# Re-ordering an edge layer's pipeline beside a dense product: two parts a step instead of three, the sum of messages last, and two masks weighted one tile ahead

## The chip, the cores and the metric

The kernel runs on one core of one Trainium2 chip. The metric is the device time of one execution in microseconds (us), taken as the median of the runs shown. TensorE (PE in the rows) does the matrix products and the transposes, VectorE (DVE) and ScalarE (ACT) the elementwise work, GpSimd (POOL) issues the gathers and scatters by index, SyncE (SP) issues the plain transfers.

## The reference, cut to what matters

A graph of 10000 nodes with 512 features and 2500 edges (sorted by `dst`) goes through four layers, each followed by a residual and a layernorm. Only the last line of the first layer and the three edge layers lie in the stretch that the change touches.

```python
x = layernorm(x + L0(x))   # two attention layers, then h @ Wfc + bfc for all nodes
x = layernorm(x + L1(x))   # relu(segment_sum((x @ weight)[src] * edge_weight, dst))
x = layernorm(x + L2(x))   # equivariant messages, src -> idx_i, dst -> idx_j:
#   hs, hv = xs @ w_in2f_s, xv @ w_in2f_v          features of a node
#   edge   = products of hs[idx_j], hv[idx_j] with a filter per edge
#   agg    = segment_sum(edge, idx_i)
#   os1, ov1 = agg @ w_f2o1 ; ssp(os1) ; @ w_f2o2
x = layernorm(x + L3(x))   # relu(concat(x[src], x[dst]) @ W.T + b), summed by src
```

A node without edges gets nothing from L1 to L3 but the layernorms, so the kernel runs the edge layers over the 20 tiles of 128 edge ends alone, and all of L0 over 79 tiles of 128 nodes.

## The kernel before, in words

The last product of L0, `h @ Wfc`, runs over the 79 node tiles one after the other (`normed_products`). A tile has eight inner blocks k = 0..7, and each block is three products of 128x512 (the operands are split in a high and a low part): lines 2597, 2598, 2599. A running number `g = 8 * tile + k` counts the blocks, and it is the clock of everything else: after block g, TensorE calls `beside(g)`, and so do ACT, DVE, POOL and SP in their own programs. What stands in `beside` is the work of the edge layers, tile by tile, laid between the blocks. Each engine runs its own list in this order and waits on semaphores, so an engine may lag behind g, but never changes the order.

Three edge layers follow each other in this frame. `conv` (L1, `ConvEdges`) starts at g = CONV = 344 and takes one step each 5 blocks. `painn` (L2, `PainnEdges`) starts at g = PAINN = 468, also at 5 blocks a step (PACE = 5), and ends near g = 598. `mlp` (L3, `MlpEdges`) loads its weights from g = MLP = 599 on, after all `painn` results have been stored, and runs on its own after the last block (g = 631).

The step n of `painn` goes from g0 = 483 + 5n. Before the change it has three parts, at g0 (part 0), g0 + 2 (part 1) and g0 + 4 (part 2). For edge tile t the chain through the engines is this:

- TensorE turns the gathered rows (`turn_x`, lines 1435 and 1438), ACT copies them out (`copy_xt`, 1505).
- TensorE makes the features (`features`, 1451: eight instructions in fp32), ACT copies them (`copy_features`, 1513).
- DVE makes the mask of equal keys (`masks`, 1587) and the messages (`messages`, 1599, 1601, 1603).
- ACT copies row 0 of the last tile's sum into row 0 of the messages (`carry`, 1520), because an edge group may run over the end of a tile.
- TensorE sums the messages by the mask (`sum_edges`, 1462), ACT copies the sums (`copy_sums`, 1528).
- TensorE turns the sums (`turn_sums`, 1469 and 1471), ACT copies them (`copy_sums_t`, 1536 and 1537).
- TensorE makes the first output product (`out_one`, 1483 and 1484), ACT copies it (`copy_hidden`, 1547 and 1548); on odd n three ACT steps make the softplus of two tiles (`softplus`, 1556 to 1560) and DVE finishes it (`scalars`, 1613).
- Two tiles later TensorE makes the second output product (`out_two`, 1494 and 1495), DVE adds the residual and takes statistics (`add`, 1621 to 1627, and on odd n `factors`, 1637), ACT makes the inverse root (`root`, 1565 and 1567), DVE the shifts (1646) and the far rows (`far`, 1653), ACT the own rows (`own`, 1573), and SP stores both (1401 and 1402).

`features` and `sum_edges` write two parts of the second half of one PSUM tensor (`e.sum_ps`, `g_sum_ps` in the rows). So `features(t)` waits for `copy_sums(t - 1)`, and `sum_edges(t)` waits for `carry(t)` and `copy_sums(t - 1)`.

DVE also serves the dense product in the same list. In an even tile it splits the next pair's operands into high and low part after k = 0, 2, 4 and 6 (lines 2839 and 2841) and at k = 2 writes the last pair's results (2968, 2976). After k = 7 of each tile it adds the residual and takes statistics (2944, 2946), and after an odd tile the spread of the pair as well (2954 to 2961). ACT does the pair's root at k = 2 of the even tile (2723, 2725).

The two weighted masks in question belong to `conv`: `weigh` (line 1286) multiplies a tile's mask by the edge weights, and `conv.sum_edges` (line 1199) is the first TensorE instruction of that layer, at g = CONV. Before the change DVE makes `weigh(0)` and `weigh(1)` at g = CONV too.

Of the kernel before, what the change touches and what calls it, by code (L numbers as in the profile page):

```python
# [33 lines left out]
ET = -(-E // P)  # L34
# [1093 lines left out]
class ConvEdges:  # L1128
# [3 lines left out]
    KC = D // P  # L1132
# [524 lines left out]
class MlpEdges:  # L1657
# [4 lines left out]
    KC = 2 * D // P  # L1662
# [207 lines left out]
def node_layers(nc, sem, held, h1, al1, scan_row, row_d, row_s, map_d, map_s, slot_tab, b1, avec, h2, h2_cols, al2, bounce1, bounce2,  # L1870
# [45 lines left out]
    def painn_part(g):  # L1916

        n, r = divmod(g - PAINN, PACE)
        return (n - 3, r // 2) if r % 2 == 0 and 0 <= n <= ET + 6 else (None, None)

    def units(m):
        return [u for u in (2 * (m % GM), 2 * (m % GM) + 1) if u < TILES]
# [44 lines left out]
    with ExitStack() as ctx:  # L1967
# [246 lines left out]
        with nc.Block() as block:  # L2214
# [303 lines left out]
            def _(pe):  # L2518
# [88 lines left out]
                def beside(g):  # L2607
                    n = conv_step(g)
                    if n is not None:
                        if 0 <= n < ET:  # L2610
                            conv.product(pe, n)
                        if 0 <= n + 1 < ET:
                            conv.turn(pe, n + 1)
                        if 0 <= n + 2 < ET:
                            conv.sum_edges(pe, n + 2)
                    n, part = painn_part(g)
                    if part == 0 and 0 <= n < ET:
                        painn.turn_sums(pe, n)
                    if part == 1:
                        if 0 <= n + 1 < ET:  # L2620
                            painn.sum_edges(pe, n + 1)
                        if 0 <= n < ET:
                            painn.out_one(pe, n)
                        if 0 <= n + 2 < ET:
                            painn.turn_x(pe, n + 2)
                        if 0 <= n - 2 < ET:
                            painn.out_two(pe, n - 2)
                    if part == 2 and 0 <= n + 2 < ET:
                        painn.features(pe, n + 2)
                    if g == FIRST_PAIR:  # L2630
                        pe.wait_ge(relu_done, turned_before(MACROS))
                        mlp.turn(pe, 0)
# [29 lines left out]
            def _(act):  # L2662
# [77 lines left out]
                def beside(g):  # L2740
# [11 lines left out]
                            conv.normalize(act, n)  # L2752
                    n, part = painn_part(g)
                    if part == 0:
                        if 0 <= n < ET:
                            painn.copy_sums_t(act, n)
                        if n % 2 == 0 and 0 <= n - 4 < ET:
                            painn.own(act, n - 4)
                    if part == 1:
                        if 0 <= n + 1 < ET:  # L2760
                            painn.copy_sums(act, n + 1)
                        if 0 <= n < ET:
                            painn.copy_hidden(act, n)
                        if 0 <= n + 2 < ET:
                            painn.copy_xt(act, n + 2)
                        if 0 <= n < ET and n % 2 == 1:
                            painn.softplus(act, n // 2)
                        if n % 2 == 0 and 0 <= n - 3 < ET:
                            painn.own(act, n - 3)
                    if part == 2:  # L2770
                        if 0 <= n + 2 < ET:
                            painn.copy_features(act, n + 2)
                            if n + 2:
                                painn.carry(act, n + 2)
                        if n % 2 == 1 and 0 <= n - 3 < ET:
                            painn.root(act, (n - 3) // 2)
                    k, r = divmod(g - MLP - MLP_PACE, MLP_PACE)
                    if r == 0 and 0 <= k < mlp.KC:
                        if k == 0:
# [44 lines left out]
            def _(dve):  # L2824
# [163 lines left out]
                def beside(g):  # L2988
# [3 lines left out]
                    if g == PAINN_W + 4 * KC:  # L2992
                        painn.scale_weights(dve)
                        dve.tensor_copy(p.side_keys[:, :], side_out[:, :, KEY]).then_inc(painn.w_scaled, 1)
                    n = conv_step(g)
                    if n is not None:
                        if n == -2:
                            conv.weigh(dve, 0)
                        if n + 3 < ET:
                            conv.weigh(dve, n + 3)  # L3000
                        if 0 <= n < ET:
                            conv.add_own(dve, n)
# [2 lines left out]
                        if 0 <= n < ET:  # L3005
                            conv.factors(dve, n)
                            conv.shifts(dve, n)
                    n, part = painn_part(g)
                    if part == 1:
                        if 0 <= n - 2 < ET:  # L3010
                            painn.add(dve, n - 2)
                        if n % 2 == 1 and 0 <= n - 3 < ET:
                            painn.factors(dve, (n - 3) // 2)
                    if part == 2:
                        if 0 <= n + 2 < ET:
                            if n == -2:
                                dve.wait_ge(painn.w_scaled, 3)
                            painn.masks(dve, n + 2)
                            painn.messages(dve, n + 2)
                        if n % 2 == 1 and 0 <= n < ET:  # L3020
                            painn.scalars(dve, n // 2)
                        if n % 2 == 1 and 0 <= n - 3 < ET:
                            painn.shifts(dve, (n - 3) // 2)
                            painn.far(dve, n - 3)
                            painn.far(dve, n - 2)
                    k, r = divmod(g - MLP - MLP_PACE, MLP_PACE)
                    if r == 0 and 0 <= k < mlp.KC:
                        mlp.rest_w(dve, k)
# [153 lines left out]
```

## Time and profile before

| what | value |
| --- | --- |
| median of 3 runs | 2332.08 us (2331.26 to 2333.86) |
| profiled execution, its own time | 2338.49 us |
| span of the profiled execution | 2336.7 us |
| PE busy | 2254.4 us (96% of the span) |
| DVE busy | 1540.6 us (66%) |
| ACT busy | 956.2 us (41%) |
| mean granted TensorE clock | 0.987 of full speed |

The profile is of one execution. It shows for each instruction its start, its duration, the idle time of its engine before it and what ended that idle time. Matmuls are pipelined, so a 128x512 product is shown as busy for 0.39 us where the next one starts 0.23 us later. What counts for TensorE is therefore the distance between starts.

### The profile page before, as it was taken

The page shows a single profiled execution, that of the slowest core. Times are in us where ns is not written, and L with a number is a line of the kernel's source. Part 1 is how long each engine was busy: PE and PEld are TensorE (multiplying, and loading weights), DVE is VectorE, ACT ScalarE, POOL GpSimd, SP SyncE. Part 2 cuts the span into 40 slices and gives each one's busy share as a digit, 9 for nine tenths or more (in the row PEclk, how much of TensorE's full clock was granted, in tenths as well). Part 3 has the DMA queues.
Part 4 walks back from the last instruction along what each step waited for, and adds up shares of the span by engine and source line. Part 5 has one row for each costly group of instructions (what it writes and reads, how often), then busy time and mean ns, then how long its engine had stood idle before and what let it go on. Part 6 is the DMA issues. An engine that isn't in the chain of part 4 may idle for free.

```text
span 2336.7 us, 36393 instructions
## 1 busy us (share of the span) xinstructions
PE 2254.4 (96%) x12307; PEld 1916.3 (82%) x12307; DVE 1540.6 (66%) x4728; ACT 956.2 (41%) x1929; POOL 943.7 (40%) x931
## 2 busy tenths in 40 slices
PE   7999999979999999999999999999999999999996
PEld 6878788868999888888999999888887777777785
DVE  7777778744666856665246664477777886778675
ACT  3982122222466522222235654334333553453353
POOL 2027637554222253565622221034435546442442
PEclk9999999989999999999999999999999999999998
DMA  6434566443576667775236764466666767665431
GB/s 205 144 131 140 154 186 208 133 139 101 166 235 232 220 204 272 265 265 178 68 120 208 244 216 168 159 211 215 209 206 221 255 224 254 193 220 169 140 120 63
DMA packets 192415, 435.82 MB, mean 187 GB/s; under 512 B 45607, under 2 KB 74542, under 8 KB 191694
## 3 DMA queue, kind: packets, MB, share of 16 engines
q1 hardware_dynamic: 126954, 249.08, 30.9%
q0 software_dynamic: 65296, 184.67, 25.4%
q8 instruction: 89, 1.46, 0.2%
q14 instruction: 76, 0.62, 0.1%
HBM read 242.68 MB, written 190.96 MB: 186 GB/s over the span
## 4 chain that ended last, share of the span: by engine, by line
PE 67%; DVE 7%; issue 2%; ACT 2%; DMA 1%; POOL 0%; DVEq 0%; ACTq 0%; POOLq 0%
PE g_h_ps L2555 6%; PE g_h_ps L2572 6%; PE g_h_ps L2557 6%; PE g_h_ps L2556 6%; PE g_h_ps L2573 6%; PE g_h_ps L2574 6%; PE g_t_ps L2534 5%; PE g_h_ps L2597 4%; PE g_h_ps L2598 4%; PE g_h_ps L2599 4%; PE g_h_ps L1742 2%; PE g_h_ps L1744 2%; PE g_h_ps L1743 2%; PE g_sum_ps L989 1%; PE g_sum_ps L990 1%
## 5 line engine op out<-in xcount | busy, mean ns | idle before, releaser
L2676 ACT ACTIVATE g_act_t<-g_t_ps,g_b_col 128x256 f32<-128x256 f32 (+1 forms) x488 | 202.6, 467 | 421.7 <-PE g_t_ps L2534 417.9
L2572 PE MATMUL g_h_ps<-g_x_hi,held_w_hi 128*128 128x256 f32 x1216 | 353.0, 290 | 0.0
L2574 PE MATMUL g_h_ps<-g_x_hi,held_w_lo 128*128 128x256 f32 x1216 | 343.9, 283 | 0.0
L2573 PE MATMUL g_h_ps<-g_x_lo,held_w_hi 128*128 128x256 f32 x1216 | 343.8, 283 | 0.0
L601 DVE CUSTOM_DVE_ANT_0 g_prod<-g_h_sb,g_a_rows 128x256 f32<-128x256 f32 x632 | 224.3, 422 | 78.6 <-ACT g_h_sb L492 71.0
L2597 PE MATMUL g_h_ps<-fc_w_hi,g_x_hi 128*128 128x512 f32 x632 | 271.9, 430 | 3.0 <-DVE fc_z L2944 2.3
L2555 PE MATMUL g_h_ps<-held_w_hi,g_x_hi 128*128 128x512 f32 x656 | 265.2, 404 | 0.0
L2557 PE MATMUL g_h_ps<-held_w_hi,g_x_lo 128*128 128x512 f32 x656 | 256.8, 391 | 0.0
L2556 PE MATMUL g_h_ps<-held_w_lo,g_x_hi 128*128 128x512 f32 x656 | 256.2, 391 | 0.0
L423 PE MATMUL g_h_ps<-g_w_hi,g_x_hi 128*128 128x512 f32 x616 | 243.3, 395 | 11.1 <-DVE g_x_lo L587 6.0
L2598 PE MATMUL g_h_ps<-fc_w_lo,g_x_hi 128*128 128x512 f32 x632 | 250.9, 397 | 0.0
L2599 PE MATMUL g_h_ps<-fc_w_hi,g_x_lo 128*128 128x512 f32 x632 | 250.9, 397 | 0.0
L2839 DVE CAST g_x_hi<-g_act_t 128x512 fp32r<-128x512 f32 (+1 forms) x244 | 104.9, 430 | 210.8 <-ACT g_act_t L2676 210.7
L424 PE MATMUL g_h_ps<-g_w_lo,g_x_hi 128*128 128x512 f32 x616 | 242.1, 393 | 0.0
L425 PE MATMUL g_h_ps<-g_w_hi,g_x_lo 128*128 128x512 f32 x616 | 241.8, 393 | 0.0
L2573 PEld LDWEIGHTS g_h_ps<-g_x_lo,held_w_hi 128*128 128x128 f32 x1216 | 233.3, 192 | 0.1
L2572 PEld LDWEIGHTS g_h_ps<-g_x_hi,held_w_hi 128*128 128x128 f32 x1216 | 233.0, 192 | 0.1
L2574 PEld LDWEIGHTS g_h_ps<-g_x_hi,held_w_lo 128*128 128x128 f32 x1216 | 232.8, 191 | 0.0
L492 ACT ACTIVATE g_h_sb<-g_h_ps 128x1024 f32<-128x1024 f32 x79 | 80.9, 1026 | 267.2 <-PE g_h_ps L425 244.3
L2857 DVE CUSTOM_DVE_ANT_0 g_prod<-g_h_sb,g_a_rows 128x256 f32<-128x256 f32 x320 | 116.6, 420 | 98.4 <-ACT g_h_sb L2696 98.2
L2387 POOL DMA_INDIRECT g_x_in<-h,held_perm x99 | 100.2, 1012 | 182.3 <-PE g_t_ps L2534 111.2
L2841 DVE TENSOR_TENSOR g_x_lo<-g_act_t,g_x_hi 128x512 fp32r<-128x512 f32 (+1 forms) x244 | 167.9, 688 | 8.4
(399 smaller groups left out, 4909.4 us busy)
## 6 DMA issues: line engine op xcount, KB each, us to landing
h<-g_h_sb SPq DMA_DIRECT2D x120, 512.0 KB, 3.8
g_x_in<-in_dram SPq DMA_DIRECT2D x40, 512.0 KB, 4.0
h<-g_rows_own SPq DMA_DIRECT2D x40, 512.0 KB, 4.9
h_cols<-g_h_sb SPq DMA_DIRECT2D x38, 512.0 KB, 5.8
xb_rows<-in_dram SPq DMA_DIRECT2D x19, 1024.0 KB
xb<-xb_rows SPq DMA_DIRECT2D x19, 1024.0 KB
g_x_in<-h_cols SPq DMA_DIRECT2D x38, 512.0 KB, 6.4
g_x_in<-h SPq DMA_DIRECT2D x21, 512.0 KB, 4.9
```

The costliest lines, as they stand in the source:

```text
L423: pe.matmul(out, xh, wh, start=(k == 0), stop=False)
L424: pe.matmul(out, xh, wl, start=False, stop=False)
L425: last = pe.matmul(out, xl, wh, start=False, stop=(k == KC - 1))
L2555: pe.matmul(out, xh, wh, start=(k == 0), stop=False)
L2556: pe.matmul(out, xh, wl, start=False, stop=False)
L2557: last = pe.matmul(out, xl, wh, start=False, stop=(k == KC - 1))
L2572: pe.matmul(out, wh, xh, start=(k == 0), stop=False)
L2573: pe.matmul(out, wh, xl, start=False, stop=False)
L2574: last = pe.matmul(out, wl, xh, start=False, stop=(k == KC - 1))
L2597: pe.matmul(out, xh, fc_hi[:, k, :], start=(k == 0), stop=False)
L2598: pe.matmul(out, xh, fc_lo[:, k, :], start=False, stop=False)
L2599: last = pe.matmul(out, xl, fc_hi[:, k, :], start=False, stop=(k == KC - 1))
```

## The change

`painn` steps get two parts instead of three: part 0 at g0 and part 1 at g0 + 3. On TensorE, part 0 is `features(n + 1)` and then `turn_sums(n)`. Part 1 is `out_one(n)`, `turn_x(n + 2)`, `out_two(n - 2)` and, last, `sum_edges(n + 1)`, which stood first in part 1 before. On ACT, `copy_sums_t(n)` now stands ahead of `carry(n + 1)`, `copy_sums` stands after the softplus, and the two `own` of a pair stand together at the end of part 1. On DVE, `masks` and `messages` move from part 2 to part 0 of the next step, with `scalars`, `shifts` and `far`. For `conv`, `weigh(0)` and `weigh(1)` move from g = CONV to g = CONV - 8, one node tile earlier. No instruction is added or removed.

```diff
-        return (n - 3, r // 2) if r % 2 == 0 and 0 <= n <= ET + 6 else (None, None)
+        return (n - 3, r // 3) if r % 3 == 0 and 0 <= n <= ET + 6 else (None, None)
... TensorE
-                    if part == 0 and 0 <= n < ET:
-                        painn.turn_sums(pe, n)
+                    if part == 0:
+                        if 0 <= n + 1 < ET:
+                            painn.features(pe, n + 1)
+                        if 0 <= n < ET:
+                            painn.turn_sums(pe, n)
                     if part == 1:
-                        if 0 <= n + 1 < ET:
-                            painn.sum_edges(pe, n + 1)
                         if 0 <= n < ET:
                             painn.out_one(pe, n)
                         if 0 <= n + 2 < ET:
                             painn.turn_x(pe, n + 2)
                         if 0 <= n - 2 < ET:
                             painn.out_two(pe, n - 2)
-                    if part == 2 and 0 <= n + 2 < ET:
-                        painn.features(pe, n + 2)
+                        if 0 <= n + 1 < ET:
+                            painn.sum_edges(pe, n + 1)
... ACT
                     if part == 0:
+                        if 0 <= n + 1 < ET:
+                            painn.copy_features(act, n + 1)
                         if 0 <= n < ET:
                             painn.copy_sums_t(act, n)
+                        if 0 < n + 1 < ET:
+                            painn.carry(act, n + 1)
                         if n % 2 == 0 and 0 <= n - 4 < ET:
-                            painn.own(act, n - 4)
+                            painn.root(act, (n - 4) // 2)
                     if part == 1:
-                        if 0 <= n + 1 < ET:
-                            painn.copy_sums(act, n + 1)
                         if 0 <= n < ET:
                             painn.copy_hidden(act, n)
                         if 0 <= n + 2 < ET:
                             painn.copy_xt(act, n + 2)
                         if 0 <= n < ET and n % 2 == 1:
                             painn.softplus(act, n // 2)
-                        if n % 2 == 0 and 0 <= n - 3 < ET:
+                        if 0 <= n + 1 < ET:
+                            painn.copy_sums(act, n + 1)
+                        if n % 2 == 0 and 0 <= n - 4 < ET:
+                            painn.own(act, n - 4)
                             painn.own(act, n - 3)
-                    if part == 2:
-                        if 0 <= n + 2 < ET:
-                            painn.copy_features(act, n + 2)
-                            if n + 2:
-                                painn.carry(act, n + 2)
-                        if n % 2 == 1 and 0 <= n - 3 < ET:
-                            painn.root(act, (n - 3) // 2)
... DVE
+                    if g == CONV - KC:
+                        conv.weigh(dve, 0)
+                        conv.weigh(dve, 1)
                     n = conv_step(g)
                     if n is not None:
-                        if n == -2:
-                            conv.weigh(dve, 0)
-                        if n + 3 < ET:
+                        if 2 <= n + 3 < ET:
                             conv.weigh(dve, n + 3)
...
                     n, part = painn_part(g)
+                    if part == 0:
+                        if n % 2 == 0 and 0 <= n - 2 < ET:
+                            painn.scalars(dve, (n - 2) // 2)
+                        if 0 <= n + 1 < ET:
+                            if n == -1:
+                                dve.wait_ge(painn.w_scaled, 3)
+                            painn.masks(dve, n + 1)
+                            painn.messages(dve, n + 1)
+                        if n % 2 == 0 and 0 <= n - 4 < ET:
+                            painn.shifts(dve, (n - 4) // 2)
+                            painn.far(dve, n - 4)
+                            painn.far(dve, n - 3)
                     if part == 1:
                         if 0 <= n - 2 < ET:
                             painn.add(dve, n - 2)
                         if n % 2 == 1 and 0 <= n - 3 < ET:
                             painn.factors(dve, (n - 3) // 2)
-                    if part == 2:
-                        if 0 <= n + 2 < ET:
-                            if n == -2:
-                                dve.wait_ge(painn.w_scaled, 3)
-                            painn.masks(dve, n + 2)
-                            painn.messages(dve, n + 2)
-                        if n % 2 == 1 and 0 <= n < ET:
-                            painn.scalars(dve, n // 2)
-                        if n % 2 == 1 and 0 <= n - 3 < ET:
-                            painn.shifts(dve, (n - 3) // 2)
-                            painn.far(dve, n - 3)
-                            painn.far(dve, n - 2)
```

## Rows read from the trace of the kernel before

**Rows 1.** The waits of TensorE: line <- released by: us in total, times, longest.
```profile
PE g_sum_ps L1462 <- ACT painn_msg L1520: 10.8, 8, 2.6
...
PE g_sum_ps L1199 <- DVE conv_weighted L1286: 3.4, 1, 3.4
...
PE g_h_ps L1494 <- issue: 1.9, 1, 1.9
PE g_misc_ps L1483 <- ACT painn_sums_t L1537: 1.6, 1, 1.6
```

**Rows 2.** Timeline of TensorE, first and last conv sum: start, duration, instruction, [idle before, releaser].
```profile
1772.52 2.07 PE L1199 MATMUL g_sum_ps<-conv_x_src,conv_weighted 128*128 128x512 f32 x2 [3.43 <-DVE conv_weighted L1286]
...
1778.08 0.40 PE L2597 MATMUL g_h_ps<-fc_w_hi,g_x_hi 128*128 128x512 f32 x1
...
1920.02 1.02 PE L1199 MATMUL g_sum_ps<-conv_x_src,conv_weighted 128*128 128x512 f32 x2
...
1922.98 0.40 PE L2597 MATMUL g_h_ps<-fc_w_hi,g_x_hi 128*128 128x512 f32 x1
```

**Rows 3.** Timeline of GpSimd: second gather of conv's tile 0.
```profile
1763.00 0.97 POOL L1182 DMA_INDIRECT conv_x_dst<-x,held_tabs  x1 [0.30 <-issue]
```

**Rows 4.** DMA issues from 1755 to 1785 us: transfer, queue, count, median us to landing.
```profile
conv_x_dst<-x,held_tabs POOLq DMA_INDIRECT x6, 4.6
...
g_a_rows<-xb,held_perm POOLq DMA_INDIRECT x2, 6.1
```

**Rows 5.** Busy time by engine in two stretches; the ninth column is the granted TensorE clock.
```profile
1770.00:1780.00 10.00, 7.48 (x22) 5.30 (x23) 2.93 (x7) 1.06 (x2) 7.56 (x9) 0.66 0.90 311
...
2020.00:2030.00 10.00, 10.00 (x50) 8.33 (x50) 7.75 (x19) 4.06 (x12) 5.65 (x6) 0.83 0.74 236
```

**Rows 6.** Timeline of TensorE: one painn step without a wait.
```profile
2024.41 0.97 PE L1451 MATMUL g_sum_ps<-painn_w_in,painn_x_t 128*128 128x32 f32 x8
...
2027.84 0.70 PE L1462 MATMUL g_sum_ps<-painn_msg,g_mask 128*128 128x320 f32 x2
2028.38 0.38 PE L1483 MATMUL g_misc_ps<-painn_sums_t,painn_o1s 128*128 128x128 f32 x2
...
2030.85 0.48 PE L2597 MATMUL g_h_ps<-fc_w_hi,g_x_hi 128*128 128x512 f32 x1
...
2031.64 0.39 PE L2597 MATMUL g_h_ps<-fc_w_hi,g_x_hi 128*128 128x512 f32 x1
...
2032.34 0.86 PE L1451 MATMUL g_sum_ps<-painn_w_in,painn_x_t 128*128 128x32 f32 x7
```

**Rows 7.** Timeline of VectorE: the list ahead of the longest wait for messages, and after it.
```profile
2010.63 0.29 DVE L1621 SCALAR_TENSOR_TENSOR painn_z<-g_h_ps,painn_z 128x128 f32<-128x128 f32 x1 [4.72 <-PE g_h_ps L1495]
...
2013.02 0.66 DVE L2944 TENSOR_TENSOR fc_z<-g_h_ps,g_a_rows 128x512 f32<-128x512 f32 x1
...
2015.40 0.43 DVE L2839 CAST g_x_hi<-g_x_in 128x512 fp32r<-128x512 f32 x1
...
2016.47 0.28 DVE L1587 TENSOR_SCALAR g_mask<-painn_key_row,painn_side_keys 128x128 fp32r<-128x128 f32 x1
...
2017.20 0.42 DVE L1613 SCALAR_TENSOR_TENSOR painn_scal<-painn_hid_s,painn_soft 128x256 f32<-128x256 f32 x1
...
2020.64 0.55 DVE L2976 TENSOR_SCALAR fc_y<-fc_z,g_rstd,g_shift 128x512 f32<-128x512 f32 x1
```

**Rows 8.** Timeline of ScalarE in the step of rows 6.
```profile
2028.58 0.44 ACT L1528 ACTIVATE painn_sums<-g_sum_ps 128x320 f32<-128x320 f32 x1 [1.01 <-PE g_sum_ps L1462]
2029.64 0.28 ACT L1547 ACTIVATE painn_hid_s<-g_misc_ps 128x128 f32<-128x128 f32 x1 [0.62 <-PE g_misc_ps L1484]
...
2031.62 0.51 ACT L1560 ACTIVATE painn_soft<-painn_soft,g_half 128x256 f32<-128x256 f32 x1
```

**Rows 9.** TensorE's groups by line: busy us, mean ns, idle before.
```profile
L1451 PE MATMUL g_sum_ps<-painn_w_in,painn_x_t 128*128 128x32 f32 x160 | 19.5, 265 | 0.0
```

**Rows 10.** Timeline of TensorE: start of the last layer.
```profile
2177.53 1.16 PE L1728 MATMUL g_t_ps<-g_ident,mlp_pair 128*128 128x128 f32 x8 [1.84 <-DVE mlp_t_lo L1820]
```

## The prediction, made before the changed kernel was run

> **What bounds the kernel now.** First the list of TensorE's waits. Nearly all of the span TensorE works, so an edit that adds and removes no instruction can gain only by waits, by order and by the clock. Two of the longer waits lie on lines that the change moves: painn's sum of messages waits 10.8 us for ACT's row copy, in 8 places, and conv's first sum waits 3.4 us for its weighted mask [rows 1]. Two more are at painn's end, 1.6 and 1.9 us [rows 1]. Then the timelines. In conv's first step TensorE runs at the lower of its two levels (1.2 instead of 2.4 GHz) after its wait: the granted clock of that stretch is 0.66, and after the longest wait for messages it is 0.83 [rows 5]. Last, the stretch behind painn: TensorE waits there for DVE before it can turn the last layer's second pair [rows 10]. A chain of stores, weight loads and splits runs from painn's last output to that point, so the end follows painn's last output, not TensorE's load after it.
>
> **conv's first masks.** DVE makes weigh(0) at g = 344 behind results, two splits and the bookkeeping of tile 42. After the change it stands eight blocks earlier, behind one split. TensorE would begin at 1772.52 - 3.43 = 1769.09. The next thing that it needs is the gathered rows of tile 0: the second gather goes out at 1763.00 [rows 3], and such gathers land 4.6 us after issue, so at 1767.6 [rows 4]. The slowest gather kind of that stretch takes 6.1 us, which gives 1769.1, still in time [rows 4]. So 3.4 us go. The lower clock goes with them: from the first sum to the third block behind it takes 1778.08 - 1772.52 = 5.56 us there and 1922.98 - 1920.02 = 2.96 us in conv's last step, so 2.6 us [rows 2]. Together 6.0 us. If the rows land 1.5 us after that (the spread between the two kinds of gather once more), 4.5 us are left. weigh is placed ahead of results on DVE, which are late by its half us; nothing waits for them there.
>
> **painn's step on TensorE.** A step without a wait takes 2032.34 - 2024.41 = 7.93 us: from features to the sum 3.43, from the sum to out_one 0.54, to the end of out_two 2.47, and two blocks, 0.79 and 0.70 [rows 6]. The first block behind fp32 work costs 0.09 more than the second. In three parts a step pays that three times, in two parts twice: 0.09 times 19 steps, 1.7 us off. Features and turn_sums take 3.43 - 2 x 0.79 - 0.70 = 1.15. So the new step reads: features at 0, three blocks, out_one at 1.15 + 0.79 + 2 x 0.70 = 3.34, the sum at 5.81, blocks from 6.35, next features at 7.84.
>
> **The cover of messages and carry.** Before, the sum came 3.43 us after its features began. DVE's list between add and messages took longer than that wherever the bookkeeping fell into it: add and factors 2.4, the tile's bookkeeping 2.4, one split 1.1, masks and messages 0.7 [rows 7]. Now the sum comes 5.81 us after its features, and DVE has 2.4 us more. To see what is left I walk DVE through the steps: each step has painn's pieces, and the fc pieces fall where 5 blocks a step meet 16 blocks a pair of tiles. Walked in the old order, with waits in steps 2, 5, 6, 9, 12, 13 and 15 of 2.1, 2.5, 0.2, 0.9, 1.6, 0.3 and 1.3 us, this gives 8.9 us of the 10.8 in the list [rows 1], so the walk reads somewhat low. Walked in the new order, the worst place is steps 5 to 7. In step 5 add ends at 8.4 after features begin (it starts at 6.05 as out_two ends), bookkeeping and split of tile 63 follow (3.5), and DVE reaches step 6 4.05 us late. Messages are done there at 5.2, and carry (taken as a copy of 0.44 [rows 8], with 0.25 to hand over) lets the sum begin 0.1 late. From there shifts, far, one split and the shifts of results take 3.4 us [rows 7] (with scalars, which now come earlier, in it), the two writes of results 0.9, and a split, add and a split 1.1 + 2.1 + 1.1. That ends at 13.7, so DVE is 5.75 late in step 7: messages at 6.55, the sum 1.5 late. There a second wait follows. ACT has carry ahead of copy_hidden, copy_xt and softplus, and from the first of these to the end of softplus takes 2032.13 - 2029.64 = 2.5 us, then copy_sums 0.44 [rows 8]; the next features wait for it, 0.7 more. All steps: 0.1, 2.2, 0.1, 0.35, 0.85 and 0.2 us in steps 6, 7, 9, 12, 13 and 17, 3.8 us. So 10.8 - 3.8 = 7.0 us go, with bounds 0 (all relocated) and 10.8. No single wait is then as long as the 2.6 us one, and the lower clock behind that one goes: 17% of 10 us [rows 5], 1.7 us, bounds 0 and 1.7.
>
> **painn's end.** The last out_two moves from g = 590 to 591, one block of 0.70 us later [rows 6]. In exchange add(16) falls behind the bookkeeping of tile 71 instead of ahead of it, so ACT's root of that pair no longer holds copy_sums_t(19): the 1.6 us go. Scalars(9) still come late, behind three splits, results and add(17): 1.3 us stay of 1.9. Sum 1.6 + 0.6 - 0.7 = 1.5 us, bounds -0.7 (both waits stay) and 2.8. own(18) moves from g = 593 to 596 together with own(19); ACT is idle there, and DVE's list is what the weight splits wait for, so this is taken as nothing, and it costs up to 0.8 us (one own) if that cover is gone.
>
> **What else is queued.** POOL's painn.gather waits for messages, now about one block later, with gathers and scatters of fc behind it; what it fetches is needed two steps later, so 15.7 us are there for three issues and a landing. On SP store(n - 4) now waits for own at the end of part 1, some 6 us later than before, with load_row and the loads of fc's columns behind it; these are due a step and 16 blocks later. ACT waits in carry for DVE, with root, copy_hidden, copy_xt and copy_sums behind it: that is the second wait above. I set POOL and SP at nothing; if a landing became late, one step would lose up to 4.6 us [rows 4].
>
> **Sum.** 6.0 + 7.0 + 1.7 + 1.7 + 1.5 = 17.9 us off. Against the profiled execution's own 2338.49 that is 2320.6. That execution is 6.4 us above the median of the runs, with the same program and the same order, so I carry the difference to the median: 2332.08 - 17.9 = 2314.2 us. With the low bounds of the likely case (conv 4.5, waits 4, clock 0, switching 1.2, end -0.7) 9.0 us go, 2323; with the high ones 6.0 + 10.8 + 1.7 + 1.7 + 2.8 = 23.0, 2309.
>
> **Rivals.** *The copy of sums becomes the wait.* Features now follow the sum after 1.5 us instead of after most of a step. Before, they never waited [rows 9]. On odd steps copy_sums stands behind softplus and ends at about 7.5 of 7.84: out_one begins at 3.34, ACT's copies 1.26 later and 2.5 us long, then 0.44, less some overlap [rows 6, 8]. If it ends 0.7 later on average than I read, ten odd steps lose 0.7 each: 7 us back, 2321. For it speaks a cover of 0.3 us; against it, that ACT is idle ahead of copy_hidden in the rows. The Trainium skill speaks for a wait here too (PSUM — Partial Sum Buffer, section "PSUM bank collisions raise a hardware error"): two engines that touch one bank must be kept apart, by bank and not by address, so the kernel can't drop it. No row before shows this wait paid. With the wait paid the sum would be 10.9 us and the time this rival's; by the rows it is 17.9.
>
> *The masks are early, but the gathered rows are not.* Then conv's first sum waits for a transfer instead, and the gain there is about 1 us instead of 6.0: 2319. Against it stand the landings above.
>
> *The waits relocate.* If DVE's list is the bound over painn, all 10.8 us come back at other lines, and the clock's 1.7 with them; conv 6.0 and switching 1.7 stay, the end loses 0.7: 7.0 us off, 2325. For it: DVE's pieces fill 80% of the new step in my walk. Against: the other 20%.
>
> *Slower: ACT and features lock.* Whenever carry ends later than about 4.6 us into an odd step, softplus and copy_sums are pushed and features wait one for one. The price is step 7's 2.2 us in each of ten odd steps and half of it in nine even ones: 32 us in place of 10.8, so 21.2 - 6.0 - 1.7 + 0.7 = 14.2 us slower, 2346. It decides from 0.94 us a step on (17.8 us over 19 steps), where all gains are used up. In my walk DVE is that late in three of 20 steps.
>
> **How the numbers follow.** Forecast (2309 to 2323) 0.59; copy of sums 0.12; gathered rows 0.08; relocation 0.14; lock 0.07. The predicted time is the forecast's, 2314.2. The range 2308 to 2324 holds the first three (0.79) and leaves out the last two. A measurement of this kernel can tell about 0.2% (4.7 us) from no change, so faster means under 2327.4 us. Forecast, copy of sums and gathered rows are all faster, and of relocation, whose size is open, two thirds (0.09): 0.88. One third of relocation is the same, 0.05. Slower is the lock, 0.07.
>
> **What would show it.** In the list of waits L1199 should be gone and the clock of conv's first 10 us stay at full. L1462 should fall from 10.8 us to 2 or less, and L1451 appear with 1 to 3 us, released by ACT's copy of sums (L1528). L1483 should be gone, L1494 be near 1.3. A step without a wait should take 7.84 us. If L1451 waits 7 us or more, the copy of sums is the wait; if L1199 waits for a transfer, the gathered rows are; if L1451, L1462 and L1494 together still have 14 us, the waits relocated. The prediction is wrong in its working if the gain comes from a place named nowhere above.

## The result, and the profile after

The changed kernel takes 2314.92 us (median; 2312.56 to 2316.88), the kernel before 2332.97 us (2331.26 to 2337.78) in the same set of runs: 18.1 us off, ratio 0.992 (95% interval 0.9904 to 0.9936). In a later set of runs it is 2315.35 against 2335.4 us, 20.1 us off, ratio 0.991 (0.989 to 0.9929). Two executions of that later set, one of the kernel before (3199 us) and one of the kernel with painn's order alone (3749 us), ran at a mean granted clock of 0.65 and 0.56, and all medians here leave them out. The prediction was 2314.2 us with 17.9 us off. The profiled execution of the changed kernel took 2312.56 us, its span is 2310.7 us.

The waits of TensorE in the changed kernel, as in [rows 1]; L1199 and L1483 are in the list no more:

```profile
PE g_t_ps L1728 <- DVE mlp_t_lo L1820: 3.4, 2, 2.2
...
PE g_sum_ps L1451 <- ACT painn_sums L1528: 1.6, 4, 0.5
...
PE g_sum_ps L1462 <- ACT painn_msg L1520: 1.0, 1, 1.0
PE g_h_ps L1494 <- issue: 1.0, 1, 1.0
```

Painn's sum of messages (L1462) waits once instead of eight times, 1.0 us instead of 10.8. The features (L1451), which had no wait before [rows 9], now wait 1.6 us for the copy of the sums: `painn_sums` is L1528. The granted clock stays at the full 2.4 GHz in the two stretches of [rows 5] (busy time by engine, the ninth column is the granted clock):

```profile
1770.00:1780.00 10.00, 10.00 (x46) 7.56 (x45) 6.96 (x20) 3.22 (x8) 7.87 (x8) 1.00 0.82 297
...
2020.00:2030.00 10.00, 10.00 (x56) 7.71 (x55) 7.72 (x23) 4.42 (x11) 3.77 (x4) 1.00 0.72 222
```

To see where the time went, the span is cut at five places that both kernels have: conv's first and last sum (L1199), painn's first `turn_x` (L1435) and last `out_two` (L1495), and the first product of the last layer (L1742). TensorE's timeline after, with the first wait of [rows 10] ahead of the last row:

```profile
1766.07 1.02 PE L1199 MATMUL g_sum_ps<-conv_x_src,conv_weighted 128*128 128x512 f32 x2
...
1910.87 1.02 PE L1199 MATMUL g_sum_ps<-conv_x_src,conv_weighted 128*128 128x512 f32 x2
...
1945.88 0.27 PE L1435 MATMUL g_sum_ps<-g_ident,painn_x 128*128 128x128 f32 x1
...
2119.41 0.39 PE L1495 MATMUL g_h_ps<-painn_o2s,painn_scal 128*128 128x128 f32 x2
...
2153.15 1.16 PE L1728 MATMUL g_t_ps<-g_ident,mlp_pair 128*128 128x128 f32 x8 [1.20 <-DVE mlp_t_lo L1820]
2154.25 0.50 PE L1742 MATMUL g_h_ps<-mlp_w_hi,mlp_t_hi 128*128 128x512 f32 x1
```

and the three rows of before that [rows 2] does not have:

```profile
1954.33 0.27 PE L1435 MATMUL g_sum_ps<-g_ident,painn_x 128*128 128x128 f32 x1
...
2143.12 0.39 PE L1495 MATMUL g_h_ps<-painn_o2s,painn_scal 128*128 128x128 f32 x2
...
2178.63 0.50 PE L1742 MATMUL g_h_ps<-mlp_w_hi,mlp_t_hi 128*128 128x512 f32 x1
```

| stretch | before, us | after, us | difference |
|---|---|---|---|
| start to where conv's first sum could begin (before: 1772.52 - 3.43) | 1769.09 | 1766.07 | -3.0 |
| conv, from there to its last sum | 150.93 | 144.80 | -6.1 |
| last conv sum to first `turn_x` | 34.31 | 35.01 | +0.7 |
| painn, first `turn_x` to last `out_two` | 188.79 | 173.53 | -15.3 |
| last `out_two` to the last layer's first product | 35.51 | 34.84 | -0.7 |
| from there to the end | 158.07 | 156.45 | -1.6 |
| sum (the spans) | 2336.7 | 2310.7 | -26.0 |

The first line and the last line of the stretches are not the change's. On TensorE the first stretch holds none of the edited work (on DVE the two masks now stand in it), and over the ten traces of this case it ends anywhere from 1765.2 to 1769.1 us, whatever the order behind it. In the second trace of the changed kernel its 1767.90 us is 1.2 below before, and the last stretch takes 157.9 us, as before. That last stretch follows the granted clock: it takes 156.1 to 156.5 us in the four traces whose clock stays full in its first 30 us, and 157.6 to 158.1 us in the six in which a window there is lower (0.83 in five of them, 0.87 and 0.95 in the kernel before). So what belongs to the change is the middle: -6.1 + 0.7 - 15.3 - 0.7 = -21.4 us in the first trace, -20.7 in the second.

### The profile page after: what moved, and what is told of

Its sections match the earlier page's. It is cut to its first block, busy times and chain, and to the rows that moved or that the text cites. A ratio compares the mean times of both kernels' runs of the same rounds, so it can differ in the third digit from the quotient of the medians.

```text
span 2310.7 us, 36393 instructions
## 1 busy us (share of the span) xinstructions
PE 2245.0 (97%) x12307; PEld 1912.7 (83%) x12307; DVE 1540.9 (67%) x4728; ACT 955.5 (41%) x1929; POOL 947.3 (41%) x931
## 4 chain that ended last, share of the span: by engine, by line
PE 68%; DVE 6%; issue 2%; ACT 2%; DMA 1%; POOL 0%; ACTq 0%; DVEq 0%; POOLq 0%
PE g_h_ps L2555 6%; PE g_h_ps L2572 6%; PE g_h_ps L2557 6%; PE g_h_ps L2556 6%; PE g_h_ps L2573 6%; PE g_h_ps L2574 6%; PE g_h_ps L2597 5%; PE g_h_ps L2598 5%; PE g_h_ps L2599 5%; PE g_t_ps L2534 5%; PE g_h_ps L1744 2%; PE g_h_ps L1742 2%; PE g_h_ps L1743 1%; PE g_sum_ps L989 1%; PE g_sum_ps L990 1%
```

## The experiments

The theory: the gain is the two listed waits (conv's first sum, painn's messages) and the time at the lower clock behind them, and both halves of painn's new order are needed, the sum last and the copy of the turned sums ahead of carry. The rivals: the gain sits in one half of the change alone; it comes from the two parts a step rather than from the order; or it comes from the run and not from the change.

### The masks alone

The kernel before, with `weigh` early:

```
+                    if g == CONV - KC:
+                        conv.weigh(dve, 0)
+                        conv.weigh(dve, 1)
                     n = conv_step(g)
                     if n is not None:
-                        if n == -2:
-                            conv.weigh(dve, 0)
-                        if n + 3 < ET:
+                        if 2 <= n + 3 < ET:
```

> The kernel before with one edit: weigh(0) and weigh(1) one node tile earlier, painn in its old three parts. My theory: conv's first sum starts about 1769 us into the span without a wait, the granted clock of the 10 us behind it stays at 1.00 where before it was 0.66, and 6.0 us go (3.4 us of wait and 2.6 us of half clock), so about 2327 us. Rival (the gathered rows are the next wait): the line of conv's first sum still waits, now released by a transfer, and 1 to 3 us go. Rival (the clock falls anyway, a little later): 3.4 us go and a stretch of granted clock well under 1.00 stands elsewhere in conv.

Measured: 2331.7 us against 2336.53, 4.8 us off where 6.0 were expected, ratio 0.998 (0.9972 to 0.9989). The wait at L1199 is gone, no window of conv is below the full clock, and conv's sums take 144.86 us from the first to the last, as in the changed kernel (before: 1920.02 - 1772.52 = 147.50). Painn keeps its old order and its waits, but they cost more in this execution: from first `turn_x` to last `out_two` it takes 191.33 us, 2.5 more than before. The windows say why. Busy time by engine, the window of its longest wait, 2.61 us:

```profile
2010.00:2020.00 10.00, 7.88 (x26) 5.73 (x27) 6.95 (x19) 4.64 (x13) 5.23 (x5) 0.66 0.52 165
```

The granted clock is 0.66 here, and 0.83 in one more window of painn: (1 - 0.66) x 10 + (1 - 0.83) x 10 = 5.1 us lost at the lower level, where the same estimate for the profiled execution of before gives 1.7 [rows 5]. The estimate can read high: for conv's first sum of before it gives 3.4 us where the timeline gives 2.6 [rows 2, 5]. The same wait in the same order had another price.

### Painn alone

The changed kernel with `weigh` where it was (the diff above, taken back), run in two sets of runs, the second of them with the changed kernel beside it.

> The changed kernel with weigh(0) and weigh(1) put back to the block of conv's first sum; painn in its new two parts. My theory: the two halves of the change do not touch each other, so about 12 us go against the kernel before (2321 us), and conv's first sum waits 3.4 us again with the clock at about 0.66 behind it. By the two traces painn alone is worth more, 14.6 us (2318 us). Rival (the halves overlap, since the same DVE lag is behind both): under 9 or over 17 us.

> The changed kernel with conv's weighted masks made where they were before, now beside the changed kernel on one chip. If the masks' 6.0 us add to painn's gain, it is 4 to 6 us slower than the changed kernel. If the order of painn takes up what the masks give (a shared wait further on), it is within 2 us of it, as the ratios of two chips (0.9923 and 0.992) seem to say.

Measured: 2318.07 against 2336.53 us, ratio 0.9923 (0.9911 to 0.9936), and 2317.63 against 2335.4, ratio 0.9925 (0.9905 to 0.9944); the changed kernel beside the second one has 2315.35. Painn's order alone is worth 17.8 to 18.5 us, more than the 12 to 14.6 expected, and in the first set more than the 17 us that stood for an overlap of the two halves. By the medians the masks add 2.3 us to it, where 4 to 6 were expected, but the intervals of the two ratios overlap (0.9905 to 0.9944 here, 0.989 to 0.9929 for the changed kernel), so the medians don't settle it. The stretches do: painn takes 173.44 and 173.43 us here and 173.53 with the masks early, and conv takes 150.87 and 148.48 us instead of 144.80 and 144.95 (from where its first sum could begin). The halves don't touch each other. The two traces also show why the masks are not worth the same 6.0 us each time. First the first one, then the second; each with the conv sum's row and the window behind it:

```profile
1768.59 2.07 PE L1199 MATMUL g_sum_ps<-conv_x_src,conv_weighted 128*128 128x512 f32 x2 [3.43 <-DVE conv_weighted L1286]
...
1770.00:1780.00 10.00, 10.00 (x36) 7.33 (x35) 2.42 (x4) 2.73 (x5) 6.33 (x7) 0.80 0.83 304
```

```profile
1769.80 1.13 PE L1199 MATMUL g_sum_ps<-conv_x_src,conv_weighted 128*128 128x512 f32 x2 [3.43 <-DVE conv_weighted L1286]
...
1770.00:1780.00 10.00, 10.00 (x43) 7.47 (x43) 3.50 (x11) 2.77 (x6) 7.21 (x8) 1.00 0.84 311
```

The wait is 3.43 us in both. In the first the clock falls with it (0.80, the sum takes 2.07 us), in the second it doesn't (1.00, 1.13 us), and conv's sums take 147.44 and 145.05 us. So the 3.4 us are there to be gained in all three traces with the masks late, the 2.6 us of low clock in two of them. The Trainium skill (TensorE: Matmul & The Clock Gate, section "What's actually happening") says that the monitor behind the clock runs freely, not from the kernel's start, so that the moment of a change shifts from run to run. These two traces of one program agree with that: one wait, one length, two outcomes. What decided between the two, no run here shows.

### The sum first, and carry first

Each undoes one half of painn's new order. On TensorE, the sum ahead of `out_one` again:

```
                     if part == 1:
+                        if 0 <= n + 1 < ET:
+                            painn.sum_edges(pe, n + 1)
                         if 0 <= n < ET:
                             painn.out_one(pe, n)
...
-                        if 0 <= n + 1 < ET:
-                            painn.sum_edges(pe, n + 1)
```

> The changed kernel with one edit: on TensorE sum_edges(n + 1) stands first in part 1 again, as in the kernel before; still two parts a step, still DVE's and ACT's new order. My theory (the cover of messages and carry is the gain): the sum comes 3.3 us after its features instead of 5.8, and the waits of L1462 for the carried row are back at about 11 us in 6 to 8 places, so 7 to 9 us slower than the changed kernel, 2322 to 2324 us. Rival (the gain is the smaller number of parts, fewer turns between fp32 and the split products, not the cover): within 1.5 us of the changed kernel, and L1462 waits 3 us or less.

On ACT, carry ahead of the copy of the turned sums:

```
+                        if 0 < n + 1 < ET:
+                            painn.carry(act, n + 1)
                         if 0 <= n < ET:
                             painn.copy_sums_t(act, n)
-                        if 0 < n + 1 < ET:
-                            painn.carry(act, n + 1)
```

> The changed kernel with one edit: on ACT carry(n + 1) stands ahead of copy_sums_t(n) again. My theory: wherever DVE is late with the messages, ACT waits in carry with the copy of the turned sums behind it, and out_one, which is due 3.3 us after features, waits for that copy: L1483 appears in the list of waits with 8 to 13 us, released by L1537, and the kernel is 6 to 10 us slower than the changed one, 2321 to 2325 us. Rival (the place of that copy is idle comfort, TensorE reaches out_one late enough): within 1.5 us of the changed kernel.

Measured: 2335.76 us, ratio 0.9992 (0.9982 to 1.0001), and 2332.77 us, ratio 0.9983 (0.9974 to 0.9993), both against 2336.53. By the ratios (0.992 and 0.991 for the changed kernel) that is 15 to 19 us slower than the changed kernel, about twice what was expected. What is left in either, 0.8 and 3.8 us, is no more than what the masks alone give: nothing of painn's gain remains. TensorE's waits, first with the sum first, then with carry first:

```profile
PE g_sum_ps L1462 <- ACT painn_msg L1520: 10.5, 8, 2.6
...
PE g_sum_ps L1451 <- ACT painn_sums L1528: 1.5, 2, 1.0
```

```profile
PE g_misc_ps L1483 <- ACT painn_sums_t L1537: 12.4, 8, 2.8
```

The mechanism is the expected one, and in both cases it is DVE's messages that are late. With the sum first TensorE meets them at the sum, as before. With carry first the sum is late enough, but ACT's queue stands still in carry, and the copy that `out_one` needs stands behind it. ACT and TensorE of that kernel at its longest wait:

```profile
2010.09 0.43 ACT L1520 ACTIVATE painn_msg<-g_sum_ps 1x320 f32<-1x320 f32 x1 [4.01 <-DVE painn_msg L1603]
2010.42 0.25 ACT L1536 ACTIVATE painn_sums_t<-g_sum_ps 128x128 f32<-128x128 f32 x1
2010.58 0.46 ACT L1537 ACTIVATE painn_sums_t<-g_sum_ps 64x384 f32<-64x384 f32 x1
...
2011.09 0.49 PE L1483 MATMUL g_misc_ps<-painn_sums_t,painn_o1s 128*128 128x128 f32 x2 [2.75 <-ACT painn_sums_t L1537]
```

What was missed is the size, and again it is the clock. Over painn the sum-first kernel takes 194.02 us, 20.5 more than the changed kernel:

```profile
1947.22 0.27 PE L1435 MATMUL g_sum_ps<-g_ident,painn_x 128*128 128x128 f32 x1
...
2141.24 0.39 PE L1495 MATMUL g_h_ps<-painn_o2s,painn_scal 128*128 128x128 f32 x2
```

Its listed waits there are 10.5 + 1.5 + 0.9 = 12.9 against 3.6, so 9.3 more. The granted clock falls behind three of them; three of the five windows that show it:

```profile
2010.00:2020.00 10.00, 9.61 (x46) 7.65 (x47) 8.95 (x23) 5.16 (x15) 5.49 (x5) 0.83 0.57 178
2040.00:2050.00 10.00, 10.00 (x43) 7.95 (x43) 4.85 (x18) 4.55 (x13) 4.26 (x5) 0.71 0.49 149
2070.00:2080.00 10.00, 7.31 (x29) 4.57 (x27) 6.88 (x18) 3.31 (x8) 2.83 (x3) 0.83 0.67 221
```

With the two others (0.95 and 0.83) that is 1.7 + 2.9 + 1.7 + 0.5 + 1.7 = 8.5 us at the lower level, in place of none. 9.3 + 8.5 = 17.8 of the 20.5 us. The carry-first kernel in the same way: 192.98 us, 11.7 us of waits more and 6.9 us by the clock, 18.6 of 19.5. So each of the two is needed, and the waits cost 1.7 to 2.2 times their listed length (19.5 / 11.7 and 20.5 / 9.3). The rest of painn's new order (DVE's messages in part 0, the places of `root`, `far` and `own`) was not run on its own; the sum-first kernel has all of it and is no faster than the kernel before.

### Three parts a step, the new order kept

```
-        return (n - 3, r // 3) if r % 3 == 0 and 0 <= n <= ET + 6 else (None, None)
+        return (n - 3, r // 2) if r % 2 == 0 and 0 <= n <= ET + 6 else (None, None)
...
-                        if 0 <= n + 1 < ET:
-                            painn.sum_edges(pe, n + 1)
+                    if part == 2 and 0 <= n + 1 < ET:
+                        painn.sum_edges(pe, n + 1)
...
+                    if part == 2 and 0 <= n + 1 < ET:
+                        painn.copy_sums(act, n + 1)
```

(ACT's `copy_sums` moves along with the sum.)

> As the changed kernel, but in three parts: features and turn_sums, two blocks, out_one to out_two, two blocks, the sum, one block. It keeps the sum last and the copy ahead of carry, and leaves out only the step in two parts. If the order of the sum and the carry is what counts, the waits stay as in the changed kernel (L1462 1 us or less, since the sum comes one block of 0.8 us later; L1451 1.6 to 8 us, since only one block instead of two lies between the sum and the next features), no window falls to the lower clock, and a step without a wait takes 0.09 us more, 7.97 instead of 7.88: 1.7 to 9 us slower than the changed kernel, and still 9 to 17 us faster than the kernel before. If the two parts are what counts, most of the 18 us is gone, and L1462 is back near 10 us.

Measured: 2317.05 us against 2335.4, ratio 0.9906 (0.9888 to 0.9925), where the changed kernel has 0.991: by the medians the two are not told apart. By the traces they are. Painn takes 177.13 us instead of 173.53, 3.6 more. A step without a wait takes 8.02 instead of 7.88 us (from `turn_x` to `turn_x`, its rows below), where 7.97 was expected; that is 19 x 0.14 = 2.7 us more. The listed waits are 5.3 us instead of 3.6, 1.7 more, and not in the places expected: L1462 has none, L1451 2.1, and two of the kernel before are there again, L1483 with 1.3 and L1494 with 1.9. Steps and waits together, 4.4 us, are a little over the 3.6 measured. The way to the first `turn_x` is 0.7 us shorter again (34.33 instead of 35.01). No window of painn is below the full clock. So it is the order that brings the gain; by the traces the two parts add some 3 us to it.

```profile
2024.27 0.33 PE L1435 MATMUL g_sum_ps<-g_ident,painn_x 128*128 128x128 f32 x1
...
2032.29 0.33 PE L1435 MATMUL g_sum_ps<-g_ident,painn_x 128*128 128x128 f32 x1
```

### The copy of sums ahead of softplus

```
+                        if 0 <= n + 1 < ET:
+                            painn.copy_sums(act, n + 1)
                         if 0 <= n < ET and n % 2 == 1:
                             painn.softplus(act, n // 2)
-                        if 0 <= n + 1 < ET:
-                            painn.copy_sums(act, n + 1)
```

> As the changed kernel, but ACT makes the copy of sums ahead of softplus and not behind it. The features' wait for that copy (L1451, 1.6 us in 4 places in the changed kernel) should go: 1 to 1.6 us faster. The copy then waits for TensorE's sum, which ends about 2.5 us after out_one's results are there, so softplus starts later by up to 2 us in every odd step. Rival: out_two, which needs softplus two steps on, is not reached by that, but turn_sums, carry and root queue behind the later softplus on ACT: then L1462 or L1494 grows by as much as L1451 loses, and the time stays or is up to 5 us worse.

> The changed kernel once more, as the base for the three kernels beside it. By the theory that its gain is the waits of conv's first sum, of painn's sum and the half clock behind them, it stays 18 to 22 us below the kernel before on this chip (ratio 0.9905 to 0.9925), with no 10 us window between conv's first step and painn's last output below a granted clock of 0.95, and the same list of waits (L1451 1.4 to 1.8 us, L1462 and L1494 near 1). By the rival, that part of the 26 us between the two profiled executions came from the run and not from the change, the ratio comes out above 0.9935.

Measured beside each other: 2312.8 us (2308.26 to 2314.77), ratio 0.9894 (0.9874 to 0.9914), and the changed kernel 2315.35 (2313.54 to 2317.04). The intervals overlap, so the medians alone don't settle it; painn's stretch does: 171.33 us, where it is 173.53 in both traces of the changed kernel and 173.44 and 173.43 in the two with the masks late. 2.2 us off, somewhat more than the 1 to 1.6 expected. Painn's first and last row there, the wait that is left, and ACT's order in an odd step:

```profile
1949.04 0.27 PE L1435 MATMUL g_sum_ps<-g_ident,painn_x 128*128 128x128 f32 x1
...
2120.37 0.39 PE L1495 MATMUL g_h_ps<-painn_o2s,painn_scal 128*128 128x128 f32 x2
```

```profile
PE g_sum_ps L1451 <- ACT painn_sums L1528: 0.5, 1, 0.5
```

```profile
2049.30 0.44 ACT L1528 ACTIVATE painn_sums<-g_sum_ps 128x320 f32<-128x320 f32 x1 [0.84 <-PE g_sum_ps L1462]
2049.63 0.41 ACT L1556 ACTIVATE painn_soft<-painn_hid_s 128x256 f32<-128x256 f32 x1
```

ACT idles 0.84 us ahead of the copy, and softplus behind it holds nothing up: L1462 and L1494 wait 1.0 and 0.9 us, as in the changed kernel. By painn's stretch this order is the best one tried.

The repeat of the changed kernel has the expected list of waits (L1451 1.6, L1462 1.0, L1494 0.9) and no window below full clock from conv's first step to painn's last output, and its ratio of 0.991 lies inside the 0.9905 to 0.9925 expected. The rival that put the gain on the run is out.

## Why the prediction was right, and which terms were not

**conv's masks** (predicted 6.0). Right in the profiled executions (150.93 - 144.80 = 6.1), and for the predicted reason: the sum at 1766.07 follows its block without a wait, so the gathered rows were there. The GpSimd queue put the second gather of tile 0 out at 1760.09, 6.0 us ahead of the sum:

```profile
1760.09 0.97 POOL L1182 DMA_INDIRECT conv_x_dst<-x,held_tabs  x1 [0.30 <-issue]
```

In the medians the term is 4.8 us with the masks alone, and 2.3, within the noise, on top of painn's order. The prediction took the low clock of one execution for a fixed price; it is one that some executions don't pay.

**painn's waits** (predicted 10.8 to 3.8). Right in the mechanism and the places, and somewhat low in the gain: the waits listed at L1462 and L1451 are 2.6 us together, so 8.2 went and not 7.0. The walk named steps 6, 7, 9, 12, 13 and 17 as late. From `turn_x` to `turn_x` the changed kernel's full steps take 7.88 us, and more only in steps 6 (8.05), 7 (9.73), 9 (8.19), 12 (8.59) and 13 (8.40), and one of the shorter first ones, which the walk didn't name, has a wait of 0.47; step 17 is not late. Together the five cost 3.6 us, 2.1 of them listed as waits at L1462 and L1451. Step 7 went as the walk had it, DVE first, then ACT, then TensorE twice, with the list of [rows 7] now ending like this:

```profile
2013.55 0.25 DVE L1603 TENSOR_TENSOR painn_msg<-painn_feat,painn_u 128x96 f32<-128x96 f32 x1
...
2013.83 0.43 ACT L1520 ACTIVATE painn_msg<-g_sum_ps 1x320 f32<-1x320 f32 x1 [4.31 <-DVE painn_msg L1603]
...
2016.47 0.42 ACT L1528 ACTIVATE painn_sums<-g_sum_ps 128x320 f32<-128x320 f32 x1
...
2014.51 0.78 PE L1462 MATMUL g_sum_ps<-painn_msg,g_mask 128*128 128x320 f32 x2 [1.02 <-ACT painn_msg L1520]
...
2017.03 1.05 PE L1451 MATMUL g_sum_ps<-painn_w_in,painn_x_t 128*128 128x32 f32 x8 [0.34 <-ACT painn_sums L1528]
```

Carry at 2013.83, then copy_hidden (at 2014.16), copy_xt and softplus, the copy of the sums at 2016.47, 2.3 us behind the start of copy_hidden (predicted 2.5, [rows 8]): 1.02 us at the sum and 0.34 at the features, where 1.5 and 0.7 were predicted.

**What a wait costs beyond its length.** This term was missing. Painn gained 15.3 us in the traces: the listed waits there went from 14.25 (10.8 + 1.6 + 1.9) to 3.55, 10.7 us; the clock gave 1.7; the step 0.6 (below). That leaves 2.3. TensorE's timeline of before around one wait shows it:

```profile
2103.74 0.40 PE L2599 MATMUL g_h_ps<-fc_w_hi,g_x_lo 128*128 128x512 f32 x1
2105.49 0.78 PE L1462 MATMUL g_sum_ps<-painn_msg,g_mask 128*128 128x320 f32 x2 [1.36 <-ACT painn_msg L1520]
2106.25 0.49 PE L1483 MATMUL g_misc_ps<-painn_sums_t,painn_o1s 128*128 128x128 f32 x2
2106.67 0.91 PE L1484 MATMUL g_misc_ps<-painn_sums_t,painn_o1v 64*128 64x384 f32 x2
```

The next instruction starts 1.75 us after the last one's start, where in a stream it is 0.23: 1.52 us late, not 1.36, since the idle time is counted from the modelled end. Then the sum takes 0.76 until `out_one` starts and `out_one` 0.42 until its second line, where a step without a wait has 0.54 [rows 6] and 2028.69 - 2028.38 = 0.31:

```profile
2028.69 0.91 PE L1484 MATMUL g_misc_ps<-painn_sums_t,painn_o1v 64*128 64x384 f32 x2
```

Together 0.16 + 0.22 + 0.11 = 0.49 us beside the listed 1.36. Over the fifteen full steps of before, which lose 14.9 us against 7.91 each, the waits listed are 9.7 and the clock 1.7; 3.4 are left for seven waits, 0.49 each. That the step behind the wait slows down is shown, and not by the clock, which is at 1.00 in that stretch (2100 to 2110 us); why TensorE restarts so slowly is not. The five late steps of the changed kernel still pay 1.5 us of this kind (3.6 lost, 2.1 listed), so 3.4 - 1.5 = 1.9 of the 2.3 us are found in the full steps.

**The clock in painn** (predicted 1.7, as an upper bound). Right for the profiled execution, too small in general: by the same estimate the old order lost 5.1 us in the trace of the kernel with the masks alone. Painn in the old order took 188.79 and 191.33 us, in the new one 173.43 to 173.53 in four traces.

**The step** (predicted 7.93 to 7.84). Overrated. TensorE's timeline of a step without a wait, as in [rows 6]:

```profile
2041.06 0.97 PE L1451 MATMUL g_sum_ps<-painn_w_in,painn_x_t 128*128 128x32 f32 x8
...
2044.45 0.38 PE L1483 MATMUL g_misc_ps<-painn_sums_t,painn_o1s 128*128 128x128 f32 x2
...
2047.00 0.70 PE L1462 MATMUL g_sum_ps<-painn_msg,g_mask 128*128 128x320 f32 x2
2047.30 0.64 PE L2597 MATMUL g_h_ps<-fc_w_hi,g_x_hi 128*128 128x512 f32 x1
...
2048.24 0.39 PE L2597 MATMUL g_h_ps<-fc_w_hi,g_x_hi 128*128 128x512 f32 x1
...
2048.94 0.97 PE L1451 MATMUL g_sum_ps<-painn_w_in,painn_x_t 128*128 128x32 f32 x8
```

`out_one` comes at 3.39 (predicted 3.34), the sum at 5.94 (5.81), the next features at 7.88 (7.84). From `turn_x` to `turn_x` most steps of before take 7.91 us, so a step gave 0.03 and the nineteen of them 0.6 us, not 1.7. The prediction carried the pieces over at the lengths they had in the old order, and they changed with their neighbours. Behind the sum the first block takes 0.94 us instead of 0.79, but the sum ahead of it only 0.30 instead of 0.54, together 0.09 less; up to `out_one` the step takes 0.05 more than predicted, and from there to the sum 2.55 instead of 2.47, 0.08 more.

**painn's end** (predicted 1.5). Right: 1.6 us at L1483 and 0.9 of the 1.9 at L1494 are gone, and the block of 0.7 us shows as the longer way to the first `turn_x` (35.01 instead of 34.31): 1.8 us. The chain behind painn gave another 0.2 to 0.7 in the two traces. The wait that stays at L1494 is 1.0 us, predicted 1.3.

**What was set at nothing.** No wait of TensorE from conv to painn's end is released by a transfer, so POOL's and SP's later issues cost nothing there.

**The rivals.** *The copy of sums becomes the wait* took place in small: L1451 waits 1.6 us where the rival needed 7, and the kernel with the copy ahead of softplus shows its full price, 2.2 us. The rule of the Trainium skill cited with it (PSUM — Partial Sum Buffer, section "PSUM bank collisions raise a hardware error") goes with a wait that stays in the kernel, and the trace agrees: even with the copy ahead of softplus 0.5 us of it is left. The order on ACT is what makes it short. *Gathered rows*, *relocation* and *lock* did not occur: no wait of conv's first sum, 3.6 us over L1451, L1462 and L1494, and in one step of twenty only the sum waits for carry.

So the change gave some 21 us in the traces, and 18.1 and 20.1 in the medians. The way from the sum to the first trace's 21.4 is 17.9 - 1.1 (the step) + 2.3 (behind the waits: the remainder above, a term that was missing) + 1.2 (the listed waits) + 0.3 (painn's end) + 0.7 (the chain behind it) + 0.1 (conv), with the clock taken from a single execution. The mechanism was right, but that 17.9 meets the first pair of medians to 0.2 us is in part luck: the sum was meant for the profiled execution, where it is 3.5 us short, and the times of the two profiled executions are 25.9 us apart (2338.49 and 2312.56).

## What to carry to other kernels

Price a wait of the engine that bounds the kernel above its listed length: here 0.5 us more for each that sits ahead of small work, and up to 3.4 us where the clock falls (the sum-first kernel's wait of 2.23 us, in two steps of 11.38 and 10.00 us against 7.88 each), which has to be looked up in several executions and not in one. When a consumer is moved later to hide its producer, move also what stands in the queues between them: with the sum last but carry ahead of the copy of turned sums, and the other way round, the whole gain of painn was gone. And a walk of one engine's list through the steps, by durations from the rows, finds the places where a wait stays, even when its sizes are off.

## What the runs showed of the hardware beyond that

A wait of 3.43 us ahead of conv's first sum was followed by the lower clock in two executions (granted clock 0.66 and 0.80 in the window) and not in a third (1.00). In the old order of painn, one and the same wait of 2.6 us cost another 2.1 us behind it in one execution (two steps of 10.99 and 9.51 us, window 0.83) and 3.4 in another (12.12 and 9.74 us, window 0.66), against 7.91 for each step. A third change between fc's blocks and painn's work in a step cost 0.14 us (8.02 against 7.88) in the new order, while the old order, with three changes too, took 7.91: here it counted which work stood beside which, and not only how many changes there were.
